# Second layer norm handed to the experts as two per-pixel rows instead of a transposed tensor

## What is computed

```python
x = x + conv_attention(ln_c(x))                 # eps 1e-6, norm over the 128 channels
t = to_tokens(x)                                # [16, 1024, 128]
n = ln_t(t)                                     # (t - mean) / sqrt(var + 1e-5), over the 128 channels
w = softmax(mean(n, axis=0) @ Wr + br)          # [1024, 8], one set for all images
h = relu(bn(n @ W1[e] + b1[e]))                 # for each expert e
h = relu(bn(h @ W2[e] + b2[e]))
t = t + sum_e w[:, e] * (h @ Wo[e] + bo[e])
```

## Time and profile before

| what | value |
|---|---|
| median of 3 runs | 819.18 us (818.71 to 819.38) |
| profiled execution, its own time | 819.31 us |
| span of the profiled execution | 817.5 us |
| mean granted TensorE clock | 0.995 of full speed |
| PE busy | 789.0 us, 97% of the span |
| DVE, ACT, POOL busy | 541.8, 423.0, 580.3 us (66%, 52%, 71%) |
| expert matmuls (L530) on the chain that ended last | 61% of the span |

### The profile page before, as it was taken

One profiled execution on the slowest core, in us unless ns is written; L12 is line 12 of the kernel. 1 busy time (PEld: TensorE's weight loads), 2 busy tenths in 40 slices (PEclk: granted clock), 3 DMA queues, 4 the chain that ended last, 5 costly groups with the idle time before them and its releaser, 6 DMA issues.

```text
span 817.5 us, 12753 instructions
## 1 busy us (share of the span) xinstructions
PE 789.0 (97%) x4186; PEld 667.5 (82%) x4186; DVE 541.8 (66%) x1053; ACT 423.0 (52%) x509; POOL 580.3 (71%) x494
## 2 busy tenths in 40 slices
PE   4999999999998889999999999999999999999997
PEld 3889999999997668888888888888888888888885
DVE  4668888787886746565665656656656566565663
ACT  3356565665655554554554545545455455454542
POOL 5447878878885368667766776677777776677665
PEclk9899999999999999999999999999999999999999
DMA  7124334443342250220201202102022020120100
GB/s 240 53 78 156 129 137 146 147 153 115 126 156 103 80 232 0 78 73 5 78 26 51 77 0 77 55 22 77 0 77 77 0 77 26 51 77 0 51 26 26
DMA packets 22107, 64.52 MB, mean 79 GB/s; under 512 B 2608, under 2 KB 6840, under 8 KB 22080
## 3 DMA queue, kind: packets, MB, share of 16 engines
q1 hardware_dynamic: 22080, 64.19, 21.6%
HBM read 38.98 MB, written 25.20 MB: 79 GB/s over the span
## 4 chain that ended last, share of the span: by engine, by line
PE 62%; DVE 2%; DMA 1%; POOL 1%; issue 1%; ACT 0%; SPq 0%; POOLq 0%; DVEq 0%
PE psum L530 61%; DMA x_res<-x_scratch 1%; POOL xn_lo L1024 1%; DVE st L858 0%; SPq L325 0%; POOLq L83 0%; POOL x_res L1055 0%; PE psum L485 0%; PE psum L586 0%; DVE xn2T L785 0%; DMA route_scratch<-routeT 0%; POOL ln L1003 0%; POOL xn2T L1011 0%; DVE x_res L964 0%; DVE w_raw L907 0%
## 5 line engine op out<-in xcount | busy, mean ns | idle before, releaser
L891 DVE SCALAR_TENSOR_TENSOR h_lo<-psum,h_hi 128x1024 fp32r<-128x1024 f32 x128 | 156.7, 1224 | 198.8 <-ACT h_hi L700 198.7
L700 ACT ACTIVATE h_hi<-psum 128x1024 fp32r<-128x1024 f32 x128 | 131.4, 1026 | 256.3 <-PE psum L530 256.3
L1024 POOL TENSOR_TENSOR h_lo<-w_raw,h_hi 128x1024 fp32r<-128x1024 f32 x64 | 154.2, 2410 | 48.7 <-ACT h_hi L712 48.7
L530 PE MATMUL psum<-h_hi,w_hi 128*128 128x512 f32 x384 | 119.4, 392 | 1.8 <-DVE w_raw L907 1.8
L907 DVE SCALAR_TENSOR_TENSOR w_raw<-psum,minus_t,route_all 128x1024 f32<-128x1024 f32 x94 | 119.9, 1275 | 1.7 <-DMA route_all<-route_scratch 1.7
L530 PE MATMUL psum<-h_hi,w_lo 128*128 128x512 f32 x384 | 119.6, 393 | 0.0
L530 PE MATMUL psum<-h_lo,w_hi 128*128 128x512 f32 x384 | 118.7, 390 | 0.0
L1024 POOL TENSOR_TENSOR xn_lo<-w_raw,xn_hi 128x1024 fp32r<-128x1024 f32 x32 | 78.0, 2438 | 51.6 <-ACT xn_hi L712 51.6
L1024 POOL TENSOR_TENSOR xn_lo<-feat_most,xn_hi 128x1024 fp32r<-128x1024 f32 x32 | 77.3, 2415 | 51.0 <-ACT xn_hi L712 51.0
L1003 POOL TENSOR_TENSOR ln<-ln,const 128x8 f32<-128x8 f32 x32 | 53.4, 1667 | 60.2 <-DVE ln L875 60.2
L530 PEld LDWEIGHTS psum<-h_hi,w_hi 128*128 128x128 f32 x384 | 71.8, 188 | 17.4 <-issue 2.6
(11 more groups left out here) (146 smaller groups left out, 1431.5 us busy)
## 6 DMA issues: line engine op xcount, KB each, us to landing
route_all<-in_x SPq DMA_DIRECT2D x16, 512.0 KB, 3.9
x_res<-in_x SPq DMA_DIRECT2D x16, 512.0 KB, 3.3
x_scratch<-x_res SPq DMA_DIRECT2D x16, 512.0 KB, 2.8
xn_scratch<-xn SPq DMA_DIRECT2D x16, 512.0 KB, 2.6
xs_in<-xn_scratch SPq DMA_DIRECT2D x16, 512.0 KB, 4.5
x_res<-x_scratch SPq DMA_DIRECT2D x16, 512.0 KB, 3.3
out<-x_res SPq DMA_DIRECT2D x15, 512.0 KB, 2.6
route_all<-route_scratch SPq DMA_DIRECT2D x6, 512.0 KB, 6.7
```

What stands on the lines that cost most here:

```text
L530: mm = pe.matmul(dst[:, px], w[:, which, e, :], part[:, px], start=first and w is w_hi and part is hi, stop=last and part is lo, skip_grou ...
L700: nc.scalar.activation(h1_hi[r][:], z1[r], ACT.Relu).then_inc(h1_hi_done, 1)
L891: nc.vector.scalar_tensor_tensor(out=h1_lo[r][:], in0=z1[r], scalar=0.0, in1=h1_hi[r][:].bitcast(F32), op0=ALU.max, op1=ALU.subtract).then ...
L1024: nc.gpsimd.tensor_tensor(h2_lo[r][:], h2w[r], h2_hi[r][:].bitcast(F32), ALU.subtract).then_inc(h2_lo_done, 1)
```

## The change

`xn2` is no longer made. SP stores the two per-pixel numbers RSTD and SHIFT of an image, 16 numbers of 4 bytes in each of 128 partitions, to `rows_dram`. It loads them back spread to 128 partitions as two tiles of 128x1024 (`rows`), and loads `xs_in` from `x1_dram`. DVE multiplies `xs_in` by the first row (`scale_xs`) and adds 1 and the second (`shift_xs`), in place. The turn of `xn2T` on PE stays for the last image alone, which `feat` needs. POOL may not write an image's two numbers before the store of the preceding image's has landed.

```diff
 # SP, step t
+                if d:
+                    sp.wait_ge(ln_done[1], t - 2)
+                    sp.dma_start(rows_dram[t - 3].rearrange("s (n p) -> p s n", p=128),
+                                 ln[1][:, RSTD:SHIFT + 1, :],
+                                 allow_slow_non_contiguous=True).then_inc(rows_stored, 16)
...
-                if at(t, IMAGES - 2):
+                if at(t, IMAGES - 3):
+                    sp.wait_ge(rows_stored, 32)
+                    load_rows(0)
                     for r in range(2):
-                        sp.wait_ge(xn2_stored[r], 16)
-                        sp.dma_start(xs_in[r][:], xn2_dram[r]).then_inc(xs_loaded[r], 16)
+                        sp.wait_ge(x1_stored[r], 16)
+                        sp.dma_start(xs_in[r][:], x1_dram[r]).then_inc(xs_loaded[r], 16)
+                if at(t, IMAGES - 1):
+                    sp.wait_ge(xs_made, 1)
+                    load_rows(1)
...
-                if d:
-                    sp.wait_ge(xn2_moved, t - 2)
-                    sp.dma_start(xn2_dram[t - 3], xn2[q][:]).then_inc(xn2_stored[q], 16)
 # PE, step t
-                if d:
-                    pe.wait_ge(norm2_first, t - 2)
-                    pe.wait_ge(norm2_last, t - 2)
-                    wait(pe, xn2_moved, t - 3)
+                if at(t, IMAGES + 2):
+                    pe.wait_ge(norm2_first, IMAGES)
+                    pe.wait_ge(norm2_last, IMAGES)
                     turn(p_chan, lambda n: xn2T[:, n, :]).then_inc(xn2t_done, 1)
 # ACT, step t
-                    nc.scalar.activation(xn2[q][:], p_chan, ACT.Copy, bias=1.0).then_inc(xn2_moved, 1)
 # DVE, end of step 14
+                if at(t, IMAGES - 2):
+                    scale_xs(0, 0)
+                    shift_xs(0, 0)
 # DVE, new
+            def scale_xs(b, p):
+                dve.wait_ge(xs_loaded[p], 8 * b + (8 if p else 16))
+                dve.wait_ge(rows_loaded, 32 * b + 32)
+                nc.vector.tensor_tensor(xs_in[p][:], xs_in[p][:], rows[0][:], ALU.mult).then_inc(xs_scaled, 1)
+            def shift_xs(b, p):
+                dve.wait_ge(xs_scaled, b + 1)
+                nc.vector.scalar_tensor_tensor(out=xs_in[p][:], in0=xs_in[p][:], scalar=1.0, in1=rows[1][:],
+                                               op0=ALU.add, op1=ALU.add).then_inc(xs_made, 1)
 # DVE, expert slots, after h1_low(s) and weigh(s - 1)
+                if k % EXPERTS == 2 and exists(s + EXPERTS):
+                    scale_xs(image + 1, 1 - k // EXPERTS)
+                if k % EXPERTS == 3 and exists(s + EXPERTS):
+                    shift_xs(image + 1, 1 - k // EXPERTS)
 # POOL, statistics
+                if k == 1:
+                    wait(pool, rows_stored, 16 * image)
```

More of the change, by code:

```diff
@@ L151, in metaformer_kernel @@
         xn2T = sb("xn2T", [128, CHUNKS, C])
-        xn2 = [sb(f"xn2_{p}", [C, PIXELS]) for p in range(2)]
+        rows = [sb(f"row_{name}", [C, PIXELS]) for name in ("rstd", "shift")]
         st = [sb(f"st{k}", [128, CHUNKS, 6]) for k in range(2)]
@@ L165, in metaformer_kernel @@
         x1_stored = [sem(f"x1_stored{p}") for p in range(2)]
-        xn2_stored = [sem(f"xn2_stored{p}") for p in range(2)]
+        rows_stored, rows_loaded = sem("rows_stored"), sem("rows_loaded")
+        xs_scaled, xs_made = sem("xs_scaled"), sem("xs_made")
         const_set = sem("const_set")
@@ L266, in slots @@
                 slot(s, s, s // EXPERTS)
-            trips = (SLOTS - first) // period
+            trips = (SLOTS - first) // period - 1
             with engine.Fori(0, trips) as i:
@@ L293, in _, with load_rows @@
                 sp.dma_start(w_raw[:, k], w.rearrange("e c h -> c e h")).then_inc(expert_w, 16)
+            def load_rows(b):
+                for k in range(2):
+                    sp.dma_start(rows[k][:], rows_dram[b, k:k + 1, :].to_broadcast([128, PIXELS])).then_inc(rows_loaded, 16)
             def step(t, p, s, a, b, c, f, d):
                 q = 1 - p
+                if d:
[3 more added lines that the diff above has]
+                                 allow_slow_non_contiguous=True).then_inc(rows_stored, 16)
                 if not isinstance(t, int) or -1 <= t < IMAGES - 3:
@@ L425, in step @@
                     pe.wait_ge(m_lo_done, t)
-                    wait(pe, xn2_moved, t - 2)
                     for n in range(2):
@@ L749, in slot @@
                     p = 1 - k // EXPERTS
-                    act.wait_ge(xs_loaded[p], 8 * image + (16 if p else 24))
+                    act.wait_ge(xs_made, image + 2)
                     wait(act, l1_done, s - 4)
@@ L781, in step @@
                     dve.wait_ge(ln_done[1], t - 2)
-                    wait(dve, xn2t_done, t - 3)
                     wait(dve, feat_done, t - 3)
@@ L922, in _ @@
             h1_low(2, 2)
-            dve.wait_ge(xn2t_done, IMAGES)
+            dve.wait_ge(xn2t_done, 1)
             dve.wait_ge(feat_most_moved, 1)
@@ L927, in _ @@
                                            op0=ALU.mult, op1=ALU.add).then_inc(feat_moved, 1)
+            scale_xs(1, 1)
             dve.wait_ge(logits_done, 1)
@@ L945, in _ @@
             h1_low(3, 3)
+            shift_xs(1, 1)
             weigh(0, 0)
@@ L1044, in step @@
                     pool.wait_ge(ln_done[1], t - 1)
-                    wait(pool, xn2t_done, t - 2)
                     wait(pool, feat_done, t - 2)
```

19 lines of the change are left out of this document (7 added, 12 removed).

## The result

The changed kernel takes 859.58 us (median of 4 runs, 859.13 to 860.44) against 819.10 for the kernel before in the same comparison: a ratio of 1.050, 95% interval 1.048 to 1.051. The forecast was 841.8, with a range of 824 to 859. The sign held, the size didn't: the loss is 40.5 us where 22.5 were forecast, and the time lies just past the upper end of the range.

The account below looks back on a forecast made before the run. PE was busy 97% of the span, but in attention ACT's exponential was taken as an equal limit. Sum: 819.31 + 0 for steady steps + 4.3 for the passage + 18.2 for the experts = 841.8 us, range 824 to 859.

Parts of the forecast that it names:

- D: Rows' store in attention: time from issue to landing, taken as 7 us, upper end 17.8; decides the last power from 5.5 on.
- Attention, gain 0: Steady attention steps: PE still waits for ACT's exponential, so removing 13.2 us of PE work gains 0.
- End of step 14: Image 0's scaling and shift on DVE ahead of step 15's `xn2T` and maximum: +2.2 us (1.9 to 2.9).
- 261.8 + 2D: Passage to the experts: earliest start of POOL's power for image 15, after waiting for the preceding images' stores.
- `bout_sb` row: Profiled load of 128 pieces of 4 bytes, 3.9 us; scaled to 2048 pieces it gave the store's upper end, 17.8 us.
- The experts: Scaling and shift on DVE for images 1 to 14: 1.3 us an image, 18.2 in all; upper bound 28.
- The exclusion: Experts: a DVE instruction with two SBUF inputs and a POOL instruction reading SBUF block each other for a whole instruction.
- The first loss: Experts: `scale_xs` waits for POOL, so `weigh` releases PE at 525.76 instead of 525.09, 0.67 us an image.
- The second: Experts: `shift_xs` waits for POOL, so the following `weigh` releases PE late, 0.64 us lost an image.
- The bound without the exclusion: Experts: only the shift and `finish` delay PE, 0.16 us an image, 2.2 us in all.
- Image 1 in the passage, 0: Passage: image 1's two instructions hide in DVE's idle time ahead of logits and first `weigh`; 0, at most 1.5 us.
- The passage: From attention to the experts: last power at 275.8 instead of 271.47, +4.3 us including step 14; range 1.4 to 12.

Follow-up runs that it names:

- the turn gone alone: Changed kernel without rows' store, loads, waits and scaling; experts use the unscaled first result, only the turn and ScalarE's copy are gone: 817.70 us, ratio 0.999.
- Long pieces: Changed kernel with the rows' store written as 256 pieces of 32 bytes instead of 2048 of 4, values landing at other pixels: 843.36 us.
- 8 columns: Changed kernel with DVE's scaling and shift for images 2 to 15 cut to 8 of 1024 columns, all waits kept: 848.91 us.
- Work without use: Useless matmuls ahead of PE's two passage waits: 858.54 us on the changed kernel, 844.13 with 32-byte store pieces, 830.38 and 820.31 on two mended versions.

## Why the prediction was wrong

By the profiled spans the sum was 18.6 us short. The step that failed first is D, taken as 7 us and measured at 10.8, which makes 7.6 of it; the clock in the passage, which had no term, makes 5.6, the experts 2.8, the traffic in the loop, also without a term, 2.6, and the start of the kernel and step 14 together about 0. The upper end of the range, 859, was 12 for the passage and 28 for the experts, and the run has 20.1 and 21.0: that it misses the range by only 0.6 us is luck.

Point by point, in the prediction's order:

- **Attention, gain 0: right.** PE's new idle time is 0.80 for a turn of 0.88, and the kernel with the turn gone alone is level with before. The reason was half right. DVE's `ctxT` releases PE there, not the exponential. And the norm on DVE ahead of the maximum, which I took for granted, was part of the ring that holds the step: with it moved, the longer steps go from 15.05 to 14.54.
- **What I left out: the store's traffic in the loop.** I treated the store as a duration that somebody may wait for. It is also 2048 packets in queues that loads need: 2.6 us in the loop of the changed kernel, and 17.1 when added to the kernel before, where it also held SP's own issues for 8 us each.
- **End of step 14: right, smaller.** +2.2 forecast; the scaling took 1.22 and the shift 1.28, neither held by POOL, and it cost 1.4.
- **D, the step that failed first.** The formula held: 261.8 + 2D with D = 10.8 gives 283.4, and 285.97 was measured, with the loop's 2.6 on top and 0.7 for the start against 0.8 less at step 14. D was mis-sized, 7 for 10.8. I took the value near the packet rate, from packets of 460 bytes, and called the `bout_sb` row an upper end. The scaled row of 4-byte pieces was the nearer kind. D of 11 stood in the range, as a bound of +12.
- **No term for the clock.** PE's waits in the passage were counted as idle time alone. Behind them PE ran near half clock and the chain took 5.6 us more, 4.8 of it on PE. Long pieces show that the clock can fall to 0.50 there without those waits, and the turn gone alone shows it at 1.00 behind the same work and the same idle times, so what lowers it stays open.
- **The experts, mechanism right, size 1.50 for 1.3.** The exclusion is shown by 8 columns that take 1.68 us, and by both instructions at 1.22 once POOL is out of the way. The first loss was near, 0.62 for 0.67. The second was put at the wrong wait: I had the next `weigh`, it was `finish`, for which `layer3` of the next image waits, and it costs 0.88, not 0.64. I listed DVE's order but not who waits for its `x_res`. That gave 21.0 for 18.2. The bound without the exclusion, 2.2, was too low for the same reason: with both instructions free 0.57 an image stay, 8.0 in all.
- **Image 1 in the passage, 0:** no row speaks against it.

The passage gave 20.1 for 4.3, of which the store's waits are 9.8, the clock and transfers 5.6, the loop 2.6, step 14 1.4, and the start of the kernel 0.7. Each stood within or near the range of its term, except the clock and the traffic, which had none. Without these two the time would have stayed inside the range.

## What to carry to other kernels

A DMA of many tiny pieces is priced by its pieces, for everyone in its queues: lay out the data so that rows are long (turn it on an engine first), and when a wait for it is taken off, look at what stands behind the pieces in the queues: of the 8.6 us by which the power came earlier 8.2 reached the experts here, but the time of the low clock wasn't won besides, since late transfers took its place. Before an instruction with two SBUF inputs, or a copy, is put on DVE, look what POOL runs at that moment, and follow its delay to every wait behind it in DVE's order, not to the next one. And compare kernels of nearly equal time with their tiles at the same addresses, or with a padding tried on both.

## What was not expected of the hardware

- The place of the operands in SBUF changes PE's pace: a shift of all later tiles by 192 bytes makes an image of the experts 0.8% faster (32.84 for 33.09 us), one by 128 bytes 1.5% slower (33.60). Which operand it is wasn't tried.
- 2048 pieces of 4 bytes stored to memory took 10.6 to 10.9 us, 5.3 ns a piece over all queues. In the kernel before with that store added, the stretch from 270 to 290 us has a DMA share of 1.10 at 89 GB/s.
- A DVE copy of 8 columns with one input took 1.86 us beside a POOL instruction.
- A backlog of such stores holds the engine that issues them: SP took 8.20 and 8.11 us for an issue of 0.43 us.
- PE's clock in the passage was 0.50 with long pieces and 1.00 with the turn gone alone, with the same work and idle times on PE in the 15 us ahead of it. Work without use kept it up there without making the kernel faster by more than 2 us.
